# Eight-column turns of equal-cell marks: whole-turn broadcast comparisons, a power-of-two column that finds the writer, and attention's closing steps two units apart

## The reference, cut to what matters

```python
# layer 0, x: (1250, 512); src, dst: (40000,), sorted by dst; edge_attr_8: (40000, 8)
xn = layernorm(x)
x = x + gnn(xn, [src, dst], edge_attr_8) + mix(xn)
# gnn: attention along the edges, a softmax over the edges of each source node
s = sum_d q[src] * k[dst] / sqrt(64) + att_bias        # 8 heads
alpha = exp(s - max) / segment_sum(exp(s - max), src)
agg = segment_sum(alpha * v[dst], src); att = agg @ Wo.T + bo
# mix: a linear attention without edges, relu features, then a feed-forward of 256
```

## Time and profile before

| | us |
|---|---|
| median of 3 runs | 2303.37 (2300.64 to 2304.42) |
| profiled execution, its own time | 2297.86 |
| span of the profile of that execution | 2296.1 |

### The profile page before, as it was taken

The page is one execution under the profiler, slowest core; times in us unless marked ns, Lnnn a source line. Parts: engine busy times, 40 slices in busy tenths (PEclk is TensorE's granted clock), DMA queues, the critical chain, the costliest instruction groups (busy, mean ns, idle before and its releaser), DMA issues.

```text
span 2296.1 us, 32035 instructions
## 1 busy us (share of the span) xinstructions
PE 2081.8 (91%) x11981; PEld 1268.9 (55%) x11981; DVE 1351.2 (59%) x4011; ACT 720.4 (31%) x1531; POOL 740.9 (32%) x525
## 2 busy tenths in 40 slices
PE   5998977798998899998999999999999999999977
PEld 3555545444335565545765456678777754455554
DVE  5666899666996976752214543441222234279997
ACT  4211222221005564432222345554211112135552
POOL 2336778887784375540000000000000000014443
PEclk9998988899998999999999999999999999999999
DMA  9994232223228997654000010002100005000000
GB/s 328 388 373 101 24 55 3 3 3 56 13 3 194 218 238 205 180 145 159 1 1 10 1 75 1 1 1 108 78 1 1 1 12 139 0 1 10 10 14 14
DMA packets 105273, 182.00 MB, mean 79 GB/s; under 512 B 64600, under 2 KB 66290, under 8 KB 94910
## 3 DMA queue, kind: packets, MB, share of 16 engines
q1 hardware_dynamic: 60047, 178.50, 24.8%
q0 software_dynamic: 45072, 1.46, 5.7%
HBM read 109.21 MB, written 70.71 MB: 78 GB/s over the span
## 4 chain that ended last, share of the span: by engine, by line
PE 61%; DVE 28%; ACT 4%; DMA 3%; issue 2%; SPq 1%; POOL 1%; ACTq 0%; DVEq 0%; PEldq 0%; POOLq 0%; PEld 0%
PE banks L203 19%; PE banks L2326 6%; PE banks L2368 6%; DVE arena L1106 5%; DVE arena L1380 4%; PE banks L1678 3%; PE banks L2154 2%; PE banks L2142 2%; PE banks L1479 2%; PE banks L2129 2%; DVE arena L481 2%; PE banks L2752 2%; PE banks L1500 2%; PE banks L197 2%; PE banks L2178 2%
## 5 line engine op out<-in xcount | busy, mean ns | idle before, releaser
L601 POOL DMA_INDIRECT edge_table<-arena x313 | 498.0, 1591 | 264.1 <-DMA edge_table<-arena 174.7
L203 PE MATMUL banks<-arena 128*125 128x512 f32 x1200 | 548.6, 604 | 16.8 <-DVE arena L2972 15.0
L203 PEld LDWEIGHTS banks<-arena 128*125 128x125 f32 x1200 | 219.2, 191 | 263.1 <-issue 244.0
L2779 POOL CAST arena<-arena 125x128 f32<-125x128 uint32 x10 | 2.9, 292 | 699.8 <-DVE arena L2915 699.6
L1380 DVE TENSOR_TENSOR arena<-banks,arena 125x1000 f32<-125x1000 f32 x100 | 192.9, 1951 | 36.0 <-ACT banks L1458 21.4
L2274 DVE SCALAR_TENSOR_TENSOR arena<-banks,arena 125x512 f32<-125x512 f32 x80 | 60.0, 751 | 189.4 <-PE banks L2368 189.4
L1415 POOL TENSOR_TENSOR arena<-arena 125x1000 f32<-125x1000 f32 x56 | 132.2, 2376 | 110.9 <-DVE arena L1380 110.6
L2021 DVE CUSTOM_DVE_ANT_0 arena<-banks,arena 125x512 f32<-125x512 f32 (+8 forms) x144 | 73.0, 553 | 128.9 <-PE banks L2129 126.1
L2326 PEld LDWEIGHTS banks<-arena 128*128 128x128 f32 x1280 | 144.0, 192 | 6.7 <-issue 6.6
L2326 PE MATMUL banks<-arena 128*128 128x125 f32 x1280 | 146.4, 276 | 0.1
L1479 PE MATMUL banks<-arena 64*125 64x250 f32 x800 | 115.3, 408 | 32.2 <-DVE arena L1380 28.4
(11 more groups left out here) (379 smaller groups left out, 3584.2 us busy)
## 6 DMA issues: line engine op xcount, KB each, us to landing
edge_table<-arena SPq DMA_DIRECT2D x23, 2304.0 KB, 21.8
arena<-edge_table SPq DMA_DIRECT2D x50, 984.4 KB
arena<-L_ffn_W SPq DMA_DIRECT2D x4, 2048.0 KB, 10.0
arena<-edge_table SPq DMA_DIRECT2D x50, 114.3 KB
adjacency<-arena SPq DMA_DIRECT2D x50, 109.4 KB
arena<-adjacency SPq DMA_DIRECT2D x10, 546.9 KB
edge_table<-arena POOLq DMA_INDIRECT x313
arena<-x SPq DMA_DIRECT2D x1, 2240.0 KB
```

The source lines that it names most:

```text
L203: last = nc.tensor.matmul(dst, xT[:, i, :], w[:, i, 0:n], start=(i == 0), stop=(i == k - 1))
L601: pool.indirect_dma_start(d["table"], bass.IndirectOffsetOnAxis(ap=cell[0:EP, c:c + 1].bitcast(U32), axis=0), vals[0:EP, c * ROW:(c + 1) * ...
```

## The change

- **Comparisons.** `mark` compares with two broadcast `tensor_tensor` operations of 1024 elements each: the even line with the even and the odd keys of all four pairs, then the odd and the next even line with the odd keys. There is no mask and no running sum any more. A `tensor_reduce` over the two odd-key blocks (1024 bf16 elements) counts, and a `scalar_tensor_tensor` (4 x 27 elements) keeps the parts of those odd edges that are not in the even column, in `kept_parts`. One semaphore step tells PE that all is there.
- **Writer by powers of two.** Each edge's parts get a 28th column that holds a power of two by its partition. The sum of it over the equal edges of a column, compared with 2.5 times the own power (`threshold`), says whether a later edge of the cell exists. This test, the counters and the address are now in `settle`, read from the sums, which now hold the full totals (nothing is added to `vals`).
- **Lines.** A ring of 17 lines (`KEY_RING`); every second turn ACT copies one more line of 128. `mark` waits for both halves of its lines before it starts, and `copy_row` waits for the comparisons alone.
- **Order.** `mark` of turn 0 moves into the layer norm's wait at the start and `settle` of turn 0 behind the normalizations. In gnn, PE spreads the lines after the k and after the v projection, in place of after q and after k; `settle` of the last turn and the count of needed columns stand between the q and k rows of the last tile. The turns are dealt to tiles by lists, still one to a tile.
- **Attention.** `DEN` is 2, `SPREAD` (4, 6), `OUT` (8, 0), and each output projection is added two units after it was issued.

```diff
+            even_lines = key_lines[0:EP, at:at + TC, :].rearrange("p (k c) n -> p k c n", c=2)[:, :, 0, :]
+            odd_lines = key_lines[0:EP, at + 1:at + 1 + TC, :].rearrange("p (k c) n -> p k (c n)", c=2)
+            both_keys = key[0:EP, TC * n:TC * (n + 1)].rearrange("p (k c) -> p k c", c=2)
+            nc.vector.tensor_tensor(equal[0:EP, :, 0:2, :], even_lines.unsqueeze(2).to_broadcast([EP, UP, 2, EP]),
+                                    both_keys.unsqueeze(3).to_broadcast([EP, UP, 2, EP]), ALU.is_equal).then_inc(s_first, 1)
+            nc.vector.tensor_tensor(equal[0:EP, :, 2:4, :].rearrange("p k b n -> p k (b n)"), odd_lines,
+                                    keys_of(n, 1).unsqueeze(2).to_broadcast([EP, UP, 2 * EP]),
+                                    ALU.is_equal).then_inc(s_first, 1)
+            dve.wait_ge(s_first, done + 2)
+            seen = flags[0:EP, :, :].rearrange("p (k c) n -> p k c n", c=2)[:, :, 1, 1:3]
+            nc.vector.tensor_reduce(seen, equal[0:EP, :, 1:4:2, :], AX_X, ALU.add).then_inc(s_first, 1)
+            dve.wait_ge(s_first, done + 3)
...
+            nc.vector.scalar_tensor_tensor(
+                out=kept_parts[0:EP, :, 0:3 * ROW], in0=seen[:, :, 0:1].to_broadcast([EP, UP, 3 * ROW]), scalar=0.0,
+                in1=odd_parts, op0=ALU.is_equal, op1=ALU.mult).then_inc(s_same, 1)
...
+        def settle(dve, n):
...
+            dve.wait_ge(s_sum, n + 1)
+            sums = sums_of(n, 0, TC)[0:EP, :].rearrange("p (c n) -> p c n", n=PART)
+            nc.vector.tensor_reduce(vals[0:EP, TC * n * ROW:TC * (n + 1) * ROW].rearrange("p (c r) -> p c r", r=ROW),
+                                    sums[:, :, 0:3 * ROW].rearrange("p c (r w) -> p c r w", w=3),
+                                    AX_X, ALU.add).then_inc(s_first, 1)
+            nc.vector.tensor_scalar(flags[0:EP, :, 0], sums[:, :, 3 * ROW], threshold[0:EP, :], None,
+                                    ALU.is_gt).then_inc(s_first, 1)
+            dve.wait_ge(s_first, done + 5)
+            nc.vector.tensor_reduce(gone[0:EP, :], flags[0:EP, :, :], AX_X, ALU.add).then_inc(s_first, 1)
+            dve.wait_ge(s_first, done + 6)
+            nc.vector.scalar_tensor_tensor(out=gone[0:EP, :], in0=gone[0:EP, :], scalar=0.0,
+                                           in1=away[0:EP, cols_n], op0=ALU.is_gt, op1=ALU.mult).then_inc(s_first, 1)
+            dve.wait_ge(s_first, done + 7)
+            nc.vector.tensor_tensor(cell[0:EP, cols_n].bitcast(U32), gone[0:EP, :], key[0:EP, cols_n],
+                                    ALU.add).then_inc(s_group, 1)
...
+            pe.wait_ge(s_same, n + 1)
...
             for k in range(UP):
...
+                add(2 * k, PART, own, even, n == 0 and k == 0, False)
+                add(2 * k, 3 * ROW, prev, odd[:, 0:3 * ROW], False, True)
+                last = add(2 * k + 1, PART, own_odd, odd, True, True)
+                if k < UP - 1 or n < TURNS - 1:
+                    last = add(2 * k + 2, PART, following, kept_parts[0:EP, k, :], True, False)
             last.then_inc(s_sum, 1)
...
+                    if j >= 1:
+                        for k in gnn_turns[t][-1:]:
+                            spread_line(pe, 2 * k + j - 1)
...
-        DEN, SPREAD, OUT = 1, (3, 5), (7, 9)
+        DEN, SPREAD, OUT = 2, (4, 6), (8, 0)
...
-                if g > CHUNKS + 1 and r == 0:
-                    add(g - CHUNKS - 2, 1)
+                if g > CHUNKS + 1:
+                    for u in range(2):
+                        if r == (OUT[u] + 2) % PER:
+                            add(g - CHUNKS - 2, u)
```

More of the change, by code:

```diff
@@ L243, in gps_two_layers @@
         away = edge.take(EC)
-        later = edge.take(2 * EP)
         spill = edge.take(2 * GE)
[L246 to L251, removed]
+        threshold, power = edge.take(1), edge.take(1)
+        equal = edge.take(UP * 4 * EP // 2).bitcast(BF16).rearrange("p (k b n) -> p k b n", k=UP, b=4)
+        kept_parts = edge.take(UP * PART // 2).bitcast(BF16).rearrange("p (k n) -> p k n", k=UP)
+        flags = edge.take(TC * 3).rearrange("p (c n) -> p c n", n=3)
+        gone = edge.take(TC)
         pair_of = edge.take(EC // 2).bitcast(BF16)
@@ new lines, in sums_of, with sum_repeats, add @@
+        def sums_of(n, a, b):
+            at = n % 2 * (BANK // 2)
+            return bank(1 if n < ATT_TURN else 7)[:, at + a * PART:at + b * PART]
+        def sum_repeats(pe, n):
+            pe.wait_ge(s_same, n + 1)
+            def add(c, width, marks_of, values, start, stop):
+                into = sums_of(n + c // TC, c % TC, c % TC + 1)[0:EP, 0:width]
+                return nc.tensor.matmul(into, marks_of, values, start=start, stop=stop, skip_group_check=True)
+            for k in range(UP):
+                even, odd = parts3[0:EP, TC * n + 2 * k, :], parts3[0:EP, TC * n + 2 * k + 1, :]
+                own, prev, own_odd, following = (equal[0:EP, k, b, :] for b in range(4))
+                add(2 * k, PART, own, even, n == 0 and k == 0, False)
[3 more added lines that the diff above has]
+                    last = add(2 * k + 2, PART, following, kept_parts[0:EP, k, :], True, False)
@@ L535, in edges_act @@
+            nc.scalar.activation(part, source, ACT.Copy).then_inc(s_part, 1)
         def edges_act(act):
@@ L714, in mix_dve @@
                                             ALU.add).then_inc(m_ev, 1)
+                    if j == 0:
+                        for k in mix_turns[t][:-1]:
+                            settle(dve, k - 1)
+                            mark(dve, k)
                 dve.wait_ge(m_ev, 3 * t + 3)
@@ L795, in mix_dve @@
                     gather_stats(Hm, t - 1)
-                settle(dve, FF_TURN + t - 1)
-                mark(dve, FF_TURN + t)
+                for k in ff_turns[t]:
+                    settle(dve, k - 1)
+                    mark(dve, k)
             dve.wait_ge(m_g, TILES)
@@ L1173, in gnn_pe @@
             pe.wait_ge(s_bias_out, BIASES)
+            for k in gnn_turns[0][:-1]:
+                for half in range(2):
+                    spread_line(pe, 2 * k + half)
             for t in range(TILES):
@@ L1395, in att_dve @@
                                 divide(g - CHUNKS - 1, half)
[L1396 to L1398 removed]
+            for u in range(2):
+                add(CHUNKS - 2, u)
             inverse(PASSES - 1)
```

309 lines of the change are left out of this document (158 added, 151 removed).

## The result

The changed kernel takes 2313.39 us (median of 13 runs, 2301.89 to 2323.49), the kernel before 2302.93 in the same session (13 runs, 2294.49 to 2307.52). The ratio is 1.0037, 95% interval 1.0024 to 1.0049: slower by 8.5 us on this ratio (5.5 to 11.3). The forecast was 2290, faster. The profiled execution took 2314.94 us for a span of 2313.1, 17.0 more than the span before.

What follows compares the result with a forecast made beforehand. DVE was taken to set the pace in the mix feed-forward, with PE nearly full in the gnn projections. Terms 0.3 - 2.3 - 4.8 - 0.3 - 6.2 = -13.3 us took the median from 2303.4 to 2290, range 2280 to 2304.

Steps and rivals of the forecast that it cites:

- rival 4: Attention starts 7 us early and finds POOL late, edge columns meeting block loads: 0 to +15 us; 0.12 with lower PE clock.
- Prices of the operations: Marks on DVE: comparisons 1.14 and 1.21 us, reduction 1.21, last operation 0.27, small ones 0.167; a turn 4.8 instead of 5.40.
- rival 1: In the marks, the counting reduction runs at L430's slower pace, 0.8 us more on 25 turns: 2310 us; chance 0.08.
- Start 0, projections +0.3: Start: extra waits covered by PE's weight wait, 0. Mix projections: longer settles and a shorter mark at the end, +0.3 us.
- Mix attention -2.3: Tiles 0 and 1 give -0.6 us, tiles 2 to 6 nothing, tiles 7 to 9 -0.58 each.
- Feed-forward -4.8: Mix feed-forward: ten turns 0.58 us shorter, the last settle +0.3, and 0.35 taken back twice by PE.
- rival 2: PE takes the marks' gain in feed-forward and mix attention: 2297 us; chance 0.08.
- gnn -0.3: Gnn projections: nine tiles at +0.03 us make +0.3, and settle and count moved in the last tile give -0.6.
- a gnn tile that grows by a microsecond: Gnn projections: one of three listed signs, any of which would make the prediction wrong.
- +0.25 of PE waiting: Each gnn tile: PE's sums end 5.35 us after settle began, against 5.08, as all 16 matmuls wait for the last step.
- Attention's ends -6.2: Two units between closing steps save 4.7 us of PE's waits at eight outputs and 1.5 of DVE's waits for denominators.
- rivals 3 and 5: 3: attention's spacing does nothing, 2296 us, 0.10 including the case with rival 2; 5: more gain than forecast, 2277, 0.07.

Runs made afterwards that it cites:

- halves: The changed kernel with each comparison of 1024 elements cut into two of 512: 2300.33 us, 0.9989 of the kernel before.
- ends_only: The kernel before with only attention's closing steps moved to the new places (two units apart): 2299.49 us, 0.9992 of the kernel before.
- keys_psum: The changed kernel with comparisons left whole but their keys copied to PSUM a turn ahead: 2292.35 us, 0.9942 of the kernel before.
- psum_again: The changed kernel with keys in PSUM and the new attention ends, measured once more in another session: 2294.44 us, 0.995 of the kernel before.

## Why the prediction was wrong

The step that failed is one that is not in the sum at all. The part on the change says what each edit does to DVE, PE and ACT; of POOL, which runs beside DVE through all four stages, it says nothing but the due times in rival 4. POOL's 1.54 us a column were taken to be its own. They are so only while DVE's instructions with two SBUF operands are short. The two comparisons made from twelve did the same work in less time, and held POOL six times as much: 21 us against 3.4.

*Rival 4* named the place and what would be late (last column, first sum of weights, 783.27 against 798.36) and had a chance of 0.12. Its cause was another one, attention starting 7 us earlier. Attention started 3.0 us earlier, and the last column 34.9 us later. Its price, up to 15 us for four more columns, was too low for the fourteen more that there were: 23.2. The rows for a better price were on hand: POOL had 13.5 us to spare, a column costs over 3 us in attention, so four columns were covered, and five, as halves showed, where 27 are left when attention begins; not fourteen. The Trainium skill ("SBUF — State Buffer", Who interferes with whom) says that a DVE instruction with two SBUF inputs contends with a GpSimd instruction that reads SBUF, and it calls the ports that they share an exclusive lock. The columns measured here, whose addresses lie in SBUF, agree: 0.73 us added on average with both operands in SBUF and none with one in PSUM. That rule spoke against this change, and it was not weighed. The same section infers that `tensor_tensor` does not hold up the descriptors that GpSimd writes for a transfer. Here it does, and the measurement decides.

The other steps, in the order of the sum:

- *Prices of the operations*: right. DVE's groups by shape in the changed kernel, to 560 us:

```profile
L493 DVE TENSOR_REDUCE arena<-arena 128x8 f32<-128x1024 bf16 x40 | 48.8, 1220 | 1.4
L486 DVE TENSOR_TENSOR arena<-arena 128x1024 bf16<-128x1024 f32 x40 | 48.7, 1219 | 0.0
L500 DVE SCALAR_TENSOR_TENSOR arena<-arena 128x108 bf16<-128x108 f32 x40 | 10.9, 274 | 1.4
L513 DVE TENSOR_SCALAR arena<-banks,arena 128x8 f32<-128x8 f32 x40 | 8.7, 219 | 0.0
```

  The forecast had 1.21, 1.21, 0.27 and 0.167 for these, so rival 1 is out. A turn takes 4.87 us, forecast 4.8.
- *Start 0, projections +0.3*: right. The first product after turn 10 is at 202.03, before at 201.68.
- *Mix attention -2.3*: +1.4. DVE's tiles are 0.53 shorter, for 0.58 forecast, but in this execution the clock stays at its lower level until 218.2 us instead of 211.6 (+2.2 by `settle` 11), as it does in ends_only with the old marks (218.7), and one tile of those with the weight product takes 11.37 instead of 10.47.
- *Feed-forward -4.8*: -5.8. A tile goes from 9.47 to 8.71 in the first half, more than the 0.58 of the turn (9.24 to 9.47 in runs with the old marks), and from 7.38 to 6.80 in the second:

```profile
393.34 0.37 DVE L510 TENSOR_REDUCE arena<-banks 128x72 f32<-128x216 f32 x1
394.38 1.22 DVE L486 TENSOR_TENSOR arena<-arena 128x1024 bf16<-128x1024 f32 x1
...
398.21 0.68 DVE L818 TENSOR_TENSOR arena<-banks,arena 125x512 f32<-125x512 f32 x1
...
400.14 0.37 DVE L510 TENSOR_REDUCE arena<-banks 128x72 f32<-128x216 f32 x1
```

  This answers to the earlier trace rows: 4.87 from `settle` to the next work, 5.40 before. Nothing was given back to PE, so rival 2 is out.
- *gnn -0.3*: +3.5 from `settle` 30 to 38. A tile takes 14.3 to 14.6, 0.2 or more above the 14.12 before, where 0.03 was forecast, and once the clock falls, 1.9: a gnn tile that grows by a microsecond was among the signs of being wrong. What was forecast as +0.25 of PE waiting was right in kind; that an unbroken wait of 1.9 us can cost more than its length was not seen.
- *Attention's ends -6.2*: 0.85 us in a late pass, 3.4 in four, for 4.7; and about 3 us in whole executions. The size is near, but the mechanism failed, so that is luck. PE's waits were to fall from 10.5 us to about 6. Over the same stretch, behind the first inversion to the end, they are 10.6. Those of 0.57 behind the outputs are gone, as forecast, and the last one fell from 1.8 to 0.45. But the waits behind the inversion, which were to stay, grew from 1.92 to 2.32, and each division has one of 0.46 now. A pass is shorter since PE's own steps follow each other faster: the closing steps now stand behind the transposes of counts (L1512, after L1578). From the start of such a transpose to the next step it is 0.48 to 0.53 us before (waits left out) and 0.31 to 0.41 after, five times a pass, and from the start of an output projection 3.64 and 3.54. Before, then after:

```profile
969.87 0.48 PE L1512 MATMUL banks<-arena 125*125 125x125 f32 x2
970.39 1.11 PE L1479 MATMUL banks<-arena 64*125 64x250 f32 x8
```
```profile
949.28 0.48 PE L1578 MATMUL banks<-arena 125*125 125x125 f32 x2
949.60 1.01 PE L1603 MATMUL banks<-arena 128*128 128x250 f32 x4
```

  Why scores follow a transpose later than a closing step does was not tried. PE in two passes of the changed kernel:

```profile
959.60 1.11 PE L1545 MATMUL banks<-arena 64*125 64x250 f32 x8 [0.46 <-DVE arena L1445]
...
984.59 1.11 PE L1545 MATMUL banks<-arena 64*125 64x250 f32 x8 [2.32 <-DVE arena L1445]
990.88 1.11 PE L1545 MATMUL banks<-arena 64*125 64x250 f32 x8 [0.46 <-DVE arena L1445]
997.15 1.11 PE L1545 MATMUL banks<-arena 64*125 64x250 f32 x8 [0.45 <-DVE arena L1445]
```

A pass did shorten and the reduction takes 1.22 us, so rivals 3 and 5 are out. With the columns no longer held, the change comes to 2292.35 and 2294.44 us (keys_psum, psum_again), near the forecast of 2290. With PE's waits filled too, which the forecast did not have, it is 2285.66 and 2295.09 in two sessions. That these surround 2290 is in part luck, since an unforeseen loss in the gnn tiles, other sizes of the ends and the unused products are in them.

## What to carry to other kernels

When DVE work is put into fewer and longer instructions, look at what POOL does meanwhile: a POOL transfer that starts in a DVE instruction with two SBUF operands waits for its end, so the price grows with the length of the single instruction (21 us held by whole comparisons, 8.1 by halves). Take one operand from PSUM, or cut the instruction. An engine that is idle 68% of the span can still be the one with a due time: work out how far it may fall behind before someone waits for it. And one longer wait of PE can cost more than several short ones, where its clock falls behind it, as in the gnn tiles here.

## What the runs showed of the hardware

- A POOL column (indirect transfer, 1.54 us) that begins in a comparison or addition with both operands in SBUF, with more than 0.13 us of it left, ends 1.41 to 1.43 us after that instruction; begun during a reduction or an addition with one operand in PSUM it takes 1.54. There are two limits. In the kernel before, thirteen columns that began in the first 0.08 us of a short comparison (0.35 or 0.48 us long) took 1.54 or 1.55, while one that began 0.04 us into a comparison of 1.22 in the changed kernel was held to its end. And a normalization (`tensor_scalar` L191, 125x512, one full operand) holds a column as well, by up to 0.25 us in the changed kernel.
- Between two comparisons POOL gets in at the end of the first. In a run of ten additions of 125x512, each with two SBUF operands, it did not: in the changed kernel one column waited through what was left of them.

```profile
562.61 6.09 DVE L1141 TENSOR_TENSOR arena<-arena 125x512 f32<-125x512 f32 x10
563.26 6.86 POOL L622 DMA_INDIRECT edge_table<-arena  x1 [0.30 <-issue]
```

  It ends at 570.12, 1.42 us after the additions do (568.70). Fourteen of the seventeen runs have one such column, of 6.2 to 7.5 us. In the other three, the kernel before among them, no column begins in that run of additions. Why the additions leave no gap was not tried.
- The same kernel differs by 5 to 23 us from run to run on one chip. In the profiled executions, part of it goes with where PE's granted clock falls to its lower level, also in parts that are the same in every kernel here: the three that took 1287 us from the last exp to the end, instead of 1276 to 1280, have it there for 10 to 21 us at 1335 to 1355 us, and no other has.
